# Two attention layers on one core: keys projected in a batch's second round, values in the fourth, the queries of the batch after in the sixth

## What is computed

```python
q = x @ Wq + bq
k = x @ Wk + bk
v = x @ Wv + bv
q = rope(q)
k = rope(k)
scores = jnp.einsum('bhqd,bhkd->bhqk', qh, kh) / jnp.sqrt(jnp.float32(HD))   # 16 heads of 8
attn = jax.nn.softmax(scores, axis=-1)
out = jnp.einsum('bhqk,bhkd->bhqd', attn, vh)
return out @ W0 + b0
# and around it
xn = _layernorm(x, axis=-1)
x = x + _L1_attn_ref(xn, ...) + _L1_ffn_ref(xn, ...)
```

## Time and profile before

| | |
|---|---|
| median of 3 executions | 3138.26 us (3138.03 to 3141.22) |
| the profiled execution, its own time | 3140.26 us |
| its span, first to last instruction | 3138.9 us |
| mean granted TensorE clock | 0.975 |
| the two layers' rounds | about 53 to 600 us of the span |
| busy in the whole span | PE 92%, DVE 77%, ACT 71%, POOL 67% |

### The profile page before, as it was taken

One profiled execution on the slowest core, in us unless ns is written; L12 is line 12 of the kernel. 1 busy time (PEld: TensorE's weight loads), 2 busy tenths in 40 slices (PEclk: granted clock), 3 DMA queues, 4 the chain that ended last, 5 costly groups with the idle time before them and its releaser, 6 DMA issues. The chain is left out here.

```text
span 3138.9 us, 72141 instructions
## 1 busy us (share of the span) xinstructions
PE 2888.9 (92%) x24662; PEld 2208.2 (70%) x24663; DVE 2418.7 (77%) x5391; ACT 2226.1 (71%) x6284; POOL 2118.3 (67%) x2393
## 2 busy tenths in 40 slices
PE   6999888887999979999979999999999999999997
PEld 4666555565888777897857777777777777777775
DVE  7788888467877764664578888888888888888887
ACT  4677777643555475465368888888888888888886
POOL 2644444236655555245069999999999999999996
PEclk7999999998999989999989999999999999999999
DMA  4222422000000011102000000000000000000001
GB/s 118 71 78 81 144 91 89 19 7 1 1 1 1 1 52 55 35 1 65 1 15 2 2 2 2 2 2 2 2 1 2 2 2 2 2 2 2 2 2 28
DMA packets 68937, 77.17 MB, mean 25 GB/s; under 512 B 8080, under 2 KB 60384, under 8 KB 68448
## 3 DMA queue, kind: packets, MB, share of 16 engines
q1 hardware_dynamic: 64976, 71.10, 7.4%
q10 hardware_dynamic: 3600, 1.46, 0.2%
HBM read 52.61 MB, written 18.87 MB: 23 GB/s over the span
## 5 line engine op out<-in xcount | busy, mean ns | idle before, releaser
L3079 POOL TENSOR_TENSOR attn_p<-attn_p,sb_few 128x512 f32<-128x512 f32 x768 | 797.5, 1054 | 109.0 <-DVE sb_few L2854 107.6
L2691 ACT ACTIVATE attn_p<-psum,sb_few 128x256 f32<-128x256 f32 x1536 | 721.4, 480 | 65.1 <-DVE sb_few L2847 65.1
L2847 DVE TENSOR_REDUCE sb_few<-psum 128x2 f32<-128x512 f32 x768 | 509.9, 678 | 14.3 <-PE psum L2545 10.4
L2563 PE MATMUL psum<-sb_kept,attn_p 128*128 128x128 f32 x3072 | 414.5, 278 | 37.5 <-DVE attn_pt L2860 30.6
L2563 PEld LDWEIGHTS psum<-sb_kept,attn_p 128*128 128x128 f32 x3072 | 332.8, 141 | 97.0 <-issue 38.3
L510 DVE TENSOR_REDUCE sb_a_nm<-psum 128x2 f32<-128x512 f32 x512 | 328.6, 684 | 79.4 <-PE psum L400 51.8
L570 ACT ACTIVATE sb_a_pt<-psum 128x512 f32<-128x512 f32 x512 | 287.7, 600 | 129.4 <-PE psum L407 64.7
L2581 PE MATMUL psum<-attn_pt,attn_v 128*64 128x256 f32 x3072 | 375.1, 386 | 0.0
L2691 ACT ACTIVATION_READ_ACCUMULATOR attn_p<-psum,sb_few 128x1 f32 x1536 | 319.3, 208 | 0.0
L2860 DVE COPY attn_pt<-psum 128x512 f32<-128x512 f32 x384 | 263.8, 687 | 32.0 <-PE psum L2563 26.3
L2581 PEld LDWEIGHTS psum<-attn_pt,attn_v 128*64 128x64 f32 x3072 | 201.7, 136 | 117.9 <-issue 32.7
(11 more groups left out here) (448 smaller groups left out, 7732.7 us busy)
## 6 DMA issues: line engine op xcount, KB each, us to landing
sb_a_spread<-a_spilled SPq DMA_DIRECT2D x64, 256.0 KB, 3.0
a_spilled<-sb_a_part_hi SPq DMA_DIRECT2D x64, 128.0 KB
a_spilled<-sb_a_part_lo SPq DMA_DIRECT2D x64, 128.0 KB
sb_a_spread<-a_spilled SPq DMA_DIRECT2D x64, 128.0 KB, 3.8
sb_gate_up<-in_L_ffn_Wg SPq DMA_DIRECT2D x32, 128.0 KB
sb_gate_up<-in_L_ffn_Wu SPq DMA_DIRECT2D x32, 128.0 KB
sb_down_w<-in_L_ffn_Wd SPq DMA_DIRECT2D x32, 128.0 KB, 2.6
sb_x<-in_L_attn_x SPq DMA_DIRECT2D x4, 512.0 KB, 7.6
```

What stands on the lines that cost most here:

```text
L2563: mm = pe.transpose(PT(e)[:, kt * N + t * P:kt * N + (t + 1) * P], Pr[p % 3][:, e, t, kt * P:(kt + 1) * P], c.ident)
L2691: ins = act.activation(Pr[p % 3][:, e, t, :], S(p, e)[:, t * N:(t + 1) * N], ACT.Exp, bias=nm[:, p % 4, e, t:t + 1], accum_out=rsum[:, p % ...
L2847: dve.tensor_reduce(nm[:, p % 4, e, :], S(p, e).rearrange("p (t n) -> p t n", t=TB), AX.X, ALU.max, negate=True).then_inc(maxed.sem, 1)
L3079: pool.tensor_tensor(P3, P3, spread(rinv[:, p % 4, e, :], N), ALU.mult).then_inc(normed[e].sem, 1)
```

## The change

The order in which `M` is passed around. The keys of batch b + 3 move from round 3 to round 1, the values of b + 1 from round 5 to round 3, and the queries are projected in round 5, of batch b + 4 in place of b + 3. The waits of each step name the reader before it in the new order. GpSimd's loop takes the parts in that order as well: keys, then maxima and the rest, and the queries' part last.

```diff
@@ project, project_v, turn_out, turn_maxima: the waits for M
-            if j and 6 <= b < B + 6:
-                pe.wait_ge(*between.moved(b - 6))
+            if j and b >= 5:
+                pe.wait_ge(*added(b - 5))
...
+            elif b >= 3:
+                pe.wait_ge(*maxima_copied(b - 3))
...
         def project_v(b):
             if b == 0:
                 pe.wait_ge(*turned_q(1))
+            elif 4 <= b < B + 4:
+                pe.wait_ge(*between.moved(b - 4))
...
         def turn_out(b):
-            if b + 2 < NB8:
-                pe.wait_ge(*v_ready(TB * (b + 3) - 1))
+            if b + 5 < NB8:
+                pe.wait_ge(*turned_q(2 * (b + 5)))
...
         def turn_maxima(b):
             pe.wait_ge(*maxima_parted(b))
...
+            pe.wait_ge(*(v_ready(TB * (b + 1) - 1) if b else turned_q(5)))
@@ TensorE's rounds
-            if j in (1, 3) and -1 <= b and b + 3 < NB8:
-                project(b + 3, j // 2)
+            if j == 1 and -1 <= b and b + 3 < NB8:
+                project(b + 3, 1)
...
-            elif j == 5 and 0 <= b and b + 1 < NB8:
+            elif j == 3 and 0 <= b and b + 1 < NB8:
                 project_v(b + 1)
+            elif j == 5 and b + 4 < NB8:
+                project(b + 4, 0)
@@ VectorE's rounds
-            elif j in (2, 4) and -1 <= b and b + 3 < NB8:
-                rope_turn(b + 3, j // 2 - 1)
-            elif j == 6 and 0 <= b and b + 1 < NB8:
+            elif j == 2 and -1 <= b and b + 3 < NB8:
+                rope_turn(b + 3, 1)
+            elif j == 4 and 0 <= b and b + 1 < NB8:
                 lay_v(b + 1, 0)
                 lay_v(b + 1, 1)
+            elif j == 6 and b + 4 < NB8:
+                rope_turn(b + 4, 0)
@@ GpSimd's loop
+        part(2, 0)
         for b in range(1, NB8 + 1):
             if b < NB8:
                 for j in range(2):
                     lay(b, j)
             if b + 1 < NB8:
-                part(b + 1, 0)
+                part(b + 1, 1)
             part_maxima(b - 1)
-            if b + 1 < NB8:
-                part(b + 1, 1)
             if b >= 3:
                 divide(b - 3)
             if 5 <= b < B + 5:
                 between.add_bias(b - 5)
             if 2 <= b <= beside.NN + 1:
                 beside.finish(b - 2)
+            if b + 2 < NB8:
+                part(b + 2, 0)
```

More of the change, by code:

```diff
@@ L320, in project_v @@
                 pe.wait_ge(*turned_q(1))
+            elif 4 <= b < B + 4:
+                pe.wait_ge(*between.moved(b - 4))
+            elif b - 1 == ternary.SUMS:
+                pe.wait_ge(*ternary.totalled(0))
+            elif b + 2 < NB8:
+                pe.wait_ge(*turned_q(2 * (b + 2) + 1))
+            elif b + 1 < NB8:
+                pe.wait_ge(*added(b - 3))
             else:
-                pe.wait_ge(*maxima_copied(b))
+                pe.wait_ge(*ternary.kept(0))
             for t in range(TB):
@@ L327, in turn_out @@
         def turn_out(b):
-            if b + 2 < NB8:
-                pe.wait_ge(*v_ready(TB * (b + 3) - 1))
+            if b + 5 < NB8:
+                pe.wait_ge(*turned_q(2 * (b + 5)))
+            elif b + 2 < NB8:
+                pe.wait_ge(*maxima_copied(b + 2))
+            elif b + 2 == NB8:
+                pe.wait_ge(*ternary.kept(1))
             else:
                 pe.wait_ge(*added(b - 1))
-                if b + 2 == NB8:
-                    pe.wait_ge(*ternary.kept(1))
             pe.wait_ge(*divided(b))
@@ L455, in pe_program @@
                 turn_back((p - 3) // 2)
-            if j in (1, 3) and -1 <= b and b + 3 < NB8:
-                project(b + 3, j // 2)
+            if j == 1 and -1 <= b and b + 3 < NB8:
+                project(b + 3, 1)
             elif j == 2 and 3 <= b < B + 3:
-                pe.wait_ge(*turned_q(2 * (b + 3)))
+                pe.wait_ge(*turned_q(2 * (b + 3) + 1))
                 between.turn(b - 3, M)
             elif j == 2 and b == ternary.SUMS:
-                pe.wait_ge(*turned_q(2 * (b + 3)))
+                pe.wait_ge(*turned_q(2 * (b + 3) + 1))
                 ternary.spread_sums(M)
```

## The result

The changed kernel takes 3145.34 us (median of 15 executions, 3143.24 to 3149.12). The kernel before takes 3138.26 (15 executions, 3136.36 to 3144.24). The ratio is 1.0020, 95% interval 1.0012 to 1.0028: slower by 7.1 us, about a third of the 22.7 us that the prediction summed up.

A forecast was written before the change was run, and what follows sets the result against it. Layer 0 was taken as bound by TensorE's idle stretches, layer 1 by the chain between TensorE and VectorE. Terms 25.6 - 5.4 + 4.6 - 2.1 gave +22.7 us, forecast 3161, own range 3152 to 3170, wider range 3142 to 3180.

The forecast's parts named there:

- The holds, +25.6: Layer 0, rounds 6 and 7: GpSimd's casts hold VectorE's small operations, delaying round 7's maxima 1.6 us in 16 batches.
- the middle, 1.6 us: Lateness assumed for round 7's maxima, between 1.2 us (one small operation held) and 2.0 us (two held).
- the tie: Third small operation due at 271.93, first cast starting at 271.9: it may be held or slip through.
- only the fourth is held: Case where the third small operation slips through: round 7's maxima start at 273.1, 1.2 us late.
- TensorE shifted by 0.2 us in rounds 5 and 6: Layer 0: `turn_out` waits for the moved rope, shifting TensorE and rounds 7 and 0 by 0.2 us.
- Collisions removed, -5.4: First four batches: the L994 pair no longer meets the small operations, returning 2.8 us of waits and 2.6 of clock.
- Layer 1, +4.6 - 2.1: Eleven batches without the norm: moved steps lengthen the chain 0.42 us each; the keys' cast is no longer waited for, saving 2.1.
- Ends, even: First queries projected early and last ones out of the tail's way: same work in two places, no net time.
- (b): Rival: casts cannot get in between the small operations and start behind the fourth; sum +1.9 us, 3140; chance 0.15.
- (c): Rival: faster, as the queries' spread lands behind the small operations, late spreads' cost returns and collisions vanish; 3131; chance 0.10.
- (a): Rival: TensorE's clock also falls after idling in round 0; 8 of 16 batches at 2.6 us, 21 more, 3182; chance 0.10.

The follow-up runs named there:

- e3: The changed kernel with GpSimd's two casts of `lay` waiting for `between.refine` of the same batch: 3137.08 us, ratio 1.0003 to the kernel before.
- e9: The changed kernel with one more small operation in `between.refine`, ahead of L221: 3171.74 us, ratio 1.0107 to the kernel before.
- e5: The changed kernel with GpSimd's casts waiting for `between.refine` and round 5's queries' projection issued ahead of `turn_back`: 3114.27 us, ratio 0.9928 to the kernel before.
- e6: The kernel before with round 5's values' projection issued ahead of `turn_back`: 3130.23 us, ratio 0.9977 to the kernel before.
- e2: The kernel before with `between.refine` moved from round 6 to the head of round 5: 3137.78 us, ratio 1.0007 to the kernel before.
- e4: The changed kernel with each of GpSimd's casts of 128x1024 made as two of 128x512: 3141.81 us, ratio 1.0019 to the kernel before.
- e12: The changed kernel with L222 split into two one-column operations and a two-column `tensor_scalar` added ahead of them: 3149.61 us, ratio 1.0050 to the kernel before.

## Why the prediction was wrong in size

The sum was 25.6 - 5.4 + 4.6 - 2.1 = 22.7. The mechanism, VectorE's small operations held by GpSimd's, is right; the size of its cost is not. By the batches' lengths of one execution each, the measured terms are these. That the time still fell into 3142 to 3180 is in part luck: two amounts that the sum doesn't have, +4.5 and -3.0 below, belong to it.

- **The holds, +25.6: the step that failed.** e3 against the changed kernel gives 0.76 to 0.81 us in ten batches, nothing in four and 0.24 in two: 8.2 in all. Three things went wrong. (1) "I take the middle, 1.6 us, since the tie may fall either way": L221 stood 0.07 to 0.08 us ahead of the cast in all ten batches, on the cheap side each time, so there is no middle; that takes 25.6 to 16 x 1.2 = 19.2. (2) "only the fourth is held: they start at 273.1, 1.2 late" was near at its place (in the changed kernel L372 of round 0 starts 8.88 us behind L352, before 7.56), but I took the lateness there for the batch's. 0.55 of the 1.3 is the longer projection and step ahead of it, and of these rounds 3 and 4, with the values' short projection, give 0.33 back. What was left is 1.01, 0.78 of it the hold: 16 x 0.78 = 12.5. (3) "`between.refine` runs in 16 batches: 16 x 1.6 = 25.6 us": only ten pay in full. In batch 12, whose rope ahead of the small operations is that of layer 1, they stand 0.1 us earlier against GpSimd:

```profile
309.31 0.58 DVE L218 TENSOR_TENSOR between_newton<-between_newton,between_rstd 128x2 f32<-128x2 f32 x1
309.93 0.16 DVE L221 SCALAR_TENSOR_TENSOR between_rstd<-between_newton,between_rstd 128x2 f32<-128x2 f32 x1
310.13 0.16 DVE L222 SCALAR_TENSOR_TENSOR between_offset<-between_mv,between_rstd 128x2 f32<-128x2 f32 x1
...
310.21 1.04 POOL L651 CAST sb_a_q<-sb_a_spread 128x1024 fp32r<-128x1024 f32 x1 [0.33 <-PE psum L406]
```

  L222 starts 0.08 us ahead of the cast and nothing is lost.
- **The order itself in the batches with a norm.** The prediction saw TensorE shifted by 0.2 us in rounds 5 and 6 and gave it no term. e3 against before gives +4.5 over these 16 (about 0.2 each in layer 0, 0.42 to 0.52 in the last five, whose rounds ahead are of layer 1).
- **Collisions removed, -5.4: right.** The two batches took 18.16 + 22.36 us before against 2 x 17.27 for ordinary ones: -6.0.
- **Layer 1, +4.6 - 2.1: the right signs, too large.** The ordinary batches are 0.16 to 0.56 longer, most of them 0.16 to 0.27 where I had 0.42, because `turn_out` starts 0.81 us later behind the maxima, and the stretch from it to the next maxima is some 0.5 shorter; I had let only part of that count. The four batches with the late cast are 0.27 to 0.43 us shorter. Over the ten: +1.4 in the changed kernel, +0.3 in e3, which lacks one batch of 16.16 us in which the clock was 0.89.
- **Ends, even: -3.0.** This is the rest of the difference of the two spans: -1.1 ahead of the first copy of maxima, +0.5 in the first three batches, -1.6 in the last two with scores, -0.8 behind the last copy. Of the -1.6, 1.3 falls in one batch in which the kernel before had a clock of 0.88, so it is not shown to come from the change.

Together 8.2 + 4.5 - 6.0 + 1.4 - 3.0 = +5.1, the difference of the two spans; with the last term as the rest, the sum is no check of the others.

Of the rivals, (b) did not occur in those ten batches: GpSimd's cast starts while L221 runs, 0.08 us behind its start, holds L222 and takes the 1.04 us that it takes elsewhere. No trace here shows GpSimd waiting for a small operation. (c) was wrong in its gate: the casts of layer 0 do not wait for their spreads. (a) stands one small operation away, as e9 shows, at 1.5 us a batch where the prediction had 2.6. The measured 0.20% is just what the prediction took for the least that a measurement tells; its interval, 1.0012 to 1.0028, still excludes a time that did not change.

## What to carry to other kernels

When a step moves, lay VectorE's small SBUF operations over GpSimd's timeline in the new order, and then ask which of them can be rid of the meeting altogether: one wait on GpSimd, where it has time, was worth 0.78 us a batch here. Carry a lateness through to the end of the period before multiplying it, and multiply it only by the periods whose timing it was worked out from. And a reorder may be worth nothing until another wait is gone: the order that lost 7 us gains 16 over the old one once the projection stands ahead of the wait for the sums and the casts are kept off the small operations (e5 against e6). Of the 13.7 us that the two layers' batches show of this in one execution each, 7.0 lie in ten batches of layer 1 and 4.4 in the two collisions that the old order has.

## What was not expected of the hardware

- A held VectorE operation ends 0.01 to 0.03 us behind GpSimd's, in e2, e4, e9 and e12 alike, and never waits beyond that one instruction, even where GpSimd's next follows at once.
- `tensor_scalar` on 128x2 with immediates is held by GpSimd and on 128x1 with scalars from a tile is not, 0.94 against 0.2 us; a reciprocal on 128x2 is not either (0.157).
- Behind a wait of TensorE of 1.50 us, the same in ten batches, its granted clock fell in eight and stayed at 1.00 in two (e9); behind waits of 0.51 us it fell in none of ten (the changed kernel).
